# Opening loads, the joint between feed-forward and second attention, and the last routing rearranged in a one-core transformer kernel

## The reference, cut to what matters

```python
x = L0_attn_x                       # (2, 512, 512): 1024 tokens, 8 tiles of 128
x = layernorm(x + L0_attention(x))  # 32 query heads of 128, 8 key/value heads, window 128, rope
x = layernorm(x + W_down(silu(x @ W_gate.T) * (x @ W_up.T)))        # hidden width 1376
x = layernorm(x + L1_attention(x))  # 32 query heads of 16, 8 key/value heads, causal, rope
x = layernorm(x + moe(x))

def moe(x):                         # 1024 tokens, E = 8 experts, top 2, lora rank 16
    h = x @ gw1.T + gb1             # width 32
    h = relu(normalise(h) * ln_gamma + ln_beta)
    gates = h @ gw2.T + gb2         # width 8: the second gate layer
    top_v, top_i = top_k(gates, 2)
    share = softmax(top_v)
    counts = number of tokens of each expert, for each of the two choices
    w = one_hot(top_i) * share * (counts <= capacity)
    low = einsum('ni,eir->enr', x, lora_A) * w      # width 8 * 16
    return x @ weight.T + low @ lora_B / 16
```

## Time and profile before

| what | value |
|---|---|
| median of 3 runs | 1286.29 us (1282.94 to 1286.7) |
| the profiled execution's own time | 1286.41 us |
| its span | 1284.6 us |
| PE busy | 1199.4 us, 93% |
| DVE busy | 810.6 us, 63% |
| ACT busy | 749.7 us, 58% |
| POOL busy | 544.0 us, 42% |
| mean granted clock of TensorE | 0.969 |

### The profile page before, as it was taken

One profiled execution on the slowest core, in us unless ns is written; L12 is line 12 of the kernel. 1 busy time (PEld: TensorE's weight loads), 2 busy tenths in 40 slices (PEclk: granted clock), 3 DMA queues, 4 the chain that ended last, 5 costly groups with the idle time before them and its releaser, 6 DMA issues. The chain is left out here.

```text
span 1284.6 us, 21017 instructions
## 1 busy us (share of the span) xinstructions
PE 1199.4 (93%) x6674; PEld 1036.9 (81%) x6674; DVE 810.6 (63%) x2534; ACT 749.7 (58%) x1739; POOL 544.0 (42%) x503
## 2 busy tenths in 40 slices
PE   6799999999999999999996999999597999999994
PEld 4688888888888888888875788878486999999883
DVE  7657776677766677666775322211655888888657
ACT  6456765566655666566653444400217999999423
POOL 4544453445543544435423233300334666676300
PEclk9899999999999999999999899999797999999997
DMA  4311110111100111011001122100201223210001
GB/s 156 105 34 41 34 34 27 35 34 34 37 24 27 42 30 46 25 26 42 2 1 33 33 73 73 57 1 1 76 22 51 49 47 105 53 39 20 1 1 66
DMA packets 30927, 52.43 MB, mean 41 GB/s; under 512 B 5728, under 2 KB 6624, under 8 KB 30816
## 3 DMA queue, kind: packets, MB, share of 16 engines
q1 hardware_dynamic: 30240, 50.02, 13.4%
q10 hardware_dynamic: 576, 1.05, 0.2%
HBM read 39.51 MB, written 2.10 MB: 32 GB/s over the span
## 5 line engine op out<-in xcount | busy, mean ns | idle before, releaser
L407 POOL TENSOR_TENSOR turned<-turned,sin 128x512 f32<-128x512 f32 x73 | 94.5, 1294 | 316.2 <-ACT turned L285 316.2
L301 ACT ACTIVATE probs<-probs,neg_max 128x256 f32<-128x256 f32 (+1 forms) x256 | 119.8, 473 | 15.8 <-DVE neg_max L493 15.8
L1335 ACT ACTIVATE a_probs<-a_probs,a_neg_max 128x512 f32<-128x512 f32 (+3 forms) x256 | 123.5, 573 | 0.0
L1536 DVE CUSTOM_DVE_ANT_0 a_probs<-bank,a_mask 128x512 f32<-128x512 f32 (+3 forms) x256 | 109.7, 484 | 1.4 <-PE bank L1737 1.1
L93 PE MATMUL bank<-wo_hi,oT_hi 128*128 128x512 f32 x256 | 101.0, 395 | 4.4 <-DVE oT_lo L555 4.4
L626 PE MATMUL bank<-xT_hi,wq_hi 128*128 128x512 f32 x256 | 102.0, 398 | 2.1 <-DVE first_by_cos L466 2.1
L410 POOL TENSOR_TENSOR turned<-turned,by_cos 128x512 f32<-128x512 f32 x73 | 100.8, 1381 | 5.7
L626 PE MATMUL bank<-xT_lo,wq_hi 128*128 128x512 f32 x256 | 100.8, 394 | 0.0
L626 PE MATMUL bank<-xT_hi,wq_lo 128*128 128x512 f32 x256 | 100.5, 393 | 0.0
L93 PE MATMUL bank<-wo_hi,oT_lo 128*128 128x512 f32 x256 | 100.4, 392 | 0.0
L93 PE MATMUL bank<-wo_lo,oT_hi 128*128 128x512 f32 x256 | 100.4, 392 | 0.0
(11 more groups left out here) (252 smaller groups left out, 3618.5 us busy)
## 6 DMA issues: line engine op xcount, KB each, us to landing
staged<-weights SPq DMA_DIRECT2D x76, 256.0 KB, 2.8
f_staged<-weights_f SPq DMA_DIRECT2D x33, 256.0 KB, 2.7
a_q_stack<-a_qT_hi SPq DMA_DIRECT2D x64, 64.0 KB, 2.0
rows<-x_rows SPq DMA_DIRECT2D x1, 2048.0 KB, 9.4
a_k_stack<-a_kT_hi SPq DMA_DIRECT2D x64, 32.0 KB, 2.0
a_q_stack<-a_qT_lo SPq DMA_DIRECT2D x32, 64.0 KB, 2.0
out<-rows SPq DMA_DIRECT2D x8, 256.0 KB, 2.0
rows<-x_T ACTq DMA_DIRECT2D x4, 256.0 KB, 5.3
```

The lines of the kernel that those rows point to most:

```text
L301: act.activation(probs[:, s % 2, h, 0:width], probs[:, s % 2, h, 0:width], ACT.Exp, bias=neg_max[:, s % 2, h:h + 1], scale=SCALE0, accum_o ...
L407: pool.tensor_tensor(at, at, sin[:, :], ALU.mult).then_inc(sin_done, 1)
L1335: act.activation(row_probs(s, qt), row_probs(s, qt), ACT.Exp, bias=neg_max[:, h, qt:qt + 1], scale=-1.0).then_inc(exp_done, 1)
L1536: dve.tensor_tensor_reduce(row_probs(s, qt), ps_s[bank][:, at:at + seen], mask[:, SEQ - seen:SEQ], -SCALE1, HIGHEST, ALU.add, ALU.min, neg ...
```

## The change

1. Opening: blocks 7 to 10 get a buffer of their own, `first_out`, which lies over the part of `wo_hi` that is filled later; SP issues their loads behind block 6 without a wait, ahead of the wait for `xT_lo_done` and of the load of `rows`. ACT waits for `rope_lo` 7 instead of 8. DVE runs `rope_low(0, 7)` and `low_values(0, 3)` ahead of `normalise(0, 1)`.
2. Joint: a new class `Ahead` places the tensors that both blocks share. In the down phase SP loads the query/key/value weights, tables and mask over the dead gate and up inputs, ACT and POOL split them, and the norm of tiles 0 to 6 runs tile by tile, one behind the matmuls; PE transposes tiles 0 to 5 between down tiles, into the space of the hidden tiles already used. The add and norm of tile 7, and the transposes of 6 and 7, are in `attention1`, whose list on PE now starts with the projection of tile 0.
3. Routing: bias, statistics, scaling run per tile (`gate_rows`, `gate_root`, `gate_scale`), the relu'd h is transposed for four tiles at a time, and the second gate layer is one PE matmul per half against a 128x32 block matrix. Top 2 and counts are per half (`choose`). `main(1)` moves behind the count matmuls, and `low` is scaled in halves. `small` is loaded with `main`.

```diff
-FIRST_PIECES = 7
+FIRST_PIECES, FIRST_OUT = 7, 7
...
+            if m >= FIRST_OUT:
+                return first_out[:, m - FIRST_OUT, :]
...
             def first_load(m):
-                if m >= FIRST_IN_PROBS + 2:
+                if FIRST_IN_PROBS + 2 <= m < FIRST_OUT:
                     sp.wait_ge(weight_lo_done, m - 1)
-                arrived = first_in[m] if m < FIRST_IN_PROBS else weight_in[m % 2]
+                arrived = first_in[m] if m < FIRST_IN_PROBS else weight_in[m % 2] if m < FIRST_OUT else out_in
...
-            first_load(6)
-            first_load(7)
+            for m in range(6, HEAD_START):
+                first_load(m)
             sp.wait_ge(xT_lo_done, 2 * KC)
             sp.dma_start(rows[:, :, :], x_rows.rearrange("(t p) d -> p t d", p=P)).then_inc(rows_in, 16)
-            for m in range(8, HEAD_START):
-                first_load(m)
...
-            act.wait_ge(rope_lo, 8)
+            act.wait_ge(rope_lo, FIRST_PIECES)
...
-            normalise(0, 1)
             rope_low(0, 7, True)
             low_values(0, 3)
+            normalise(0, 1)
...
+class Ahead:
+        self.at, self.weights_at, self.banks = at, weights_at, banks
+        self.xT = put("xT", [P, KC, 2, TOK], at, F32R)
+        self.xT_hi, self.xT_lo = self.xT[:, :, 0, :], self.xT[:, :, 1, :]
...
+    def add_row(self, dve, rows, norm, tile):
+        dve.wait_ge(self.y_ready, tile + 1)
+        dve.tensor_tensor(rows[:, tile, :], self.banks[tile % 2][:, :], rows[:, tile, :], ALU.add).then_inc(self.y_added, 1)
+        dve.wait_ge(self.y_added, tile + 1)
+        norm.take(dve, tile)
+        norm.moments(dve, tile)
...
+            sp.wait_ge(up_ready, 2 * F_TILES)
+            for k in range(KC):
+                sp.dma_start(ahead.raw[:, k, :], w_qkv[k]).then_inc(ahead.weight_in[k], 16)
+            sp.dma_start(ahead.cos[:, :, :], cos_in).then_inc(ahead.constants_in, 16)
+            sp.dma_start(ahead.sin[:, :, :], sin_in).then_inc(ahead.constants_in, 16)
+            sp.dma_start(ahead.mask[:, :], mask_in).then_inc(ahead.constants_in, 16)
...
+            for k in range(KC):
+                act.wait_ge(ahead.weight_in[k], 16)
+                act.activation(ahead.w_hi[:, k, :], ahead.raw[:, k, :], ACT.Copy).then_inc(ahead.w_hi_done, 1)
+            for tile in range(TILES - 1):
+                if tile >= 1:
+                    next_norm.high(act, tile - 1)
+                next_norm.root(act, tile)
...
+            for k in range(KC):
+                pool.wait_ge(ahead.w_hi_done, k + 1)
+                pool.tensor_tensor(ahead.w_lo[:, k, :], ahead.raw[:, k, :], ahead.w_hi[:, k, :].bitcast(F32),
+                                   ALU.subtract).then_inc(ahead.w_lo_done, 1)
...
-            for tile in range(TILES):
-                dve.wait_ge(y_ready, tile + 1)
-                dve.tensor_tensor(rows[:, tile, :], ps_y[tile % 2][:, :], rows[:, tile, :],
-                                  ALU.add).then_inc(y_added, 1)
-                dve.wait_ge(y_added, tile + 1)
-                next_norm.take(dve, tile)
+            for tile in range(TILES - 1):
+                ahead.add_row(dve, rows, next_norm, tile)
+                if tile >= 1:
+                    next_norm.split_low(dve, tile - 1)
+                next_norm.scale(dve, tile)
...
+                if 1 <= tile < TILES - 1:
+                    next_norm.turn(pe, tile - 1)
...
+        norm = t["norms"][1]
-        ps_q, ps_kv, ps_part = psum[0:2], psum[2:4], psum[6:8]
+        ps_q, ps_kv, ps_part = psum[2:4], psum[6:8], psum[4:6]
...
+        ps_hT = [psum[1][:, 0:P], psum[6][:, 0:P]]
+        ps_gates = [psum[1][:, P:P + 4 * EXPERTS], psum[6][:, P:P + 4 * EXPERTS]]
+        ps_count = psum[6][:, 2 * P:2 * P + 2 * EXPERTS]
...
-            norm.on_scalar(act, transposed=False)
-            high_weight(0)
-            for tile in range(TILES):
-                if tile < KC - 1:
-                    high_weight(tile + 1)
-                act.wait_ge(norm.turned, tile + 1)
-                act.activation(xT_hi[:, :, tile * P:(tile + 1) * P], norm.bank(tile), ACT.Copy).then_inc(norm.hi_done, 1)
-
+            norm.root(act, TILES - 1)
...
+                if tile < 2:
+                    norm.high(act, TILES - 2 + tile)
...
+            def gate_root(tile):
+                act.wait_ge(var_ready, tile + 1)
+                act.activation(dev[:, tile:tile + 1], h_moments[:, tile, 1:2], ACT.Sqrt,
+                               bias=norm.eps[:, 0:1]).then_inc(dev_done, 1)
+
+            def turned_gates(part):
+
+                act.wait_ge(gate_steps, 2 * part + 1)
+                act.activation(hT[:, part, :], ps_hT[part], ACT.Relu).then_inc(hT_done, 1)
...
+                if tile >= 3:
+                    gate_root(tile - 3)
...
+            turned_gates(0)
+            gate_root(TILES - 3)
             norm2.high(act, TILES - 1)
             low_rows(TILES - 2)
+            gate_root(TILES - 2)
             low_rows(TILES - 1)
-            act.wait_ge(var_ready, 1)
-            act.activation(dev[:, :], var[:, :], ACT.Sqrt, bias=norm.eps[:, 0:1],
-                           scale=1.0 / GATE_H).then_inc(dev_done, 1)
-            act.wait_ge(gap_ready, 1)
-            act.activation(share[:, 1, :], gap[:, :], ACT.Exp).then_inc(share_done, 1)
+            gate_root(TILES - 1)
+            turned_gates(1)
+            act.wait_ge(choice_done, 3)
+            act.activation(share[:, 1, :], gap[:, :], ACT.Exp).then_inc(dev_done, 1)
...
-            weights(range(KC))
...
-            norm.on_vector(dve)
+            ahead.add_row(dve, rows, norm, TILES - 1)
+            norm.scale(dve, TILES - 1)
...
+                if tile < 2:
+                    norm.split_low(dve, TILES - 2 + tile)
...
+            def gate_rows(tile):
+                dve.wait_ge(side_ready, tile + 1)
+                dve.tensor_tensor(h[:, tile, :], ps_side[tile % 2][:, 0:GATE_H], names["gb1"], ALU.add).then_inc(h_copied, 1)
+                dve.wait_ge(h_copied, tile + 1)
+                step(dve.bn_stats(h_stats[:, tile, :], h[:, tile, :]))
+                dve.bn_aggr(h_moments[:, tile, :], h_stats[:, tile, :]).then_inc(var_ready, 1)
+
+            def gate_scale(tile):
+                dve.wait_ge(dev_done, tile + 1)
+                step(dve.reciprocal(dev[:, tile:tile + 1], dev[:, tile:tile + 1]))
+                step(dve.tensor_scalar(h[:, tile, :], h[:, tile, :], h_moments[:, tile, 0:1], dev[:, tile:tile + 1],
+                                       ALU.subtract, ALU.mult))
+                step(dve.tensor_tensor(h[:, tile, :], h[:, tile, :], names["gamma"], ALU.mult))
+                dve.tensor_tensor(h[:, tile, :], h[:, tile, :], names["beta"], ALU.add).then_inc(h_done, 1)
+
+            def choose(part):
+
+                tiles = range(4 * part, 4 * part + 4)
+                some = slice(4 * part, 4 * part + 4)
+                dve.wait_ge(gate_steps, 2 * part + 2)
+                step(dve.tensor_tensor(gates[:, some, :], ps_gates[part].rearrange("p (t e) -> p t e", e=EXPERTS),
+                                       each_of(names["gb2"], 4, EXPERTS), ALU.add))
+                for tile in tiles:
+                    found = dve.max(top[:, tile, :], gates[:, tile, :])
+                step(found)
+                for tile in tiles:
+                    found = dve.max_index(top_index[:, tile, :], top[:, tile, :], gates[:, tile, :])
+                step(found)
+                step(dve.tensor_copy(top_at[:, some, :], top_index[:, some, :]))
+                dve.tensor_tensor(gap[:, some], top[:, some, 1], top[:, some, 0], ALU.subtract).then_inc(choice_done, 1)
+                for n in range(2):
+                    found = dve.tensor_tensor(chosen[:, n, some, :], each_column(top_at[:, some, n], EXPERTS, 4),
+                                              each_of(names["index"], 4, EXPERTS), ALU.is_equal)
+                step(found)
+                dve.tensor_reduce(count[:, part, :, :].rearrange("p n e -> p (n e)"),
+                                  chosen[:, :, some, :].rearrange("p n t e -> p n e t"), mybir.AxisListType.X,
+                                  ALU.add).then_inc(choice_done, 1)
...
+            dve.wait_ge(main_in, 48)
+                if tile >= 3:
+                    gate_scale(tile - 3)
             norm2.split_low(dve, TILES - 2)
             gate_rows(TILES - 3)
+            choose(0)
+            gate_scale(TILES - 3)
             norm2.split_low(dve, TILES - 1)
             gate_rows(TILES - 2)
+            gate_scale(TILES - 2)
             gate_rows(TILES - 1)
...
+            gate_scale(TILES - 1)
+            choose(1)
...
+            for part in range(2):
+                some = slice(4 * part, 4 * part + 4)
+                by_expert = low[:, some, :].rearrange("p t (e r) -> p (t e) r", r=RANK)
+                dve.tensor_tensor(by_expert, by_expert,
```

(71 more changed lines are left out.)

189 lines of the change are left out of this document (77 added, 112 removed).

## The result

The changed kernel takes 1256.12 us (median of 4 runs, 1254.46 to 1256.77) against 1285.32 us for the kernel before on the same chip (4 runs, 1282.94 to 1286.7): ratio 0.9774, 95% interval 0.9758 to 0.9791. The forecast was 1257, the range 1251 to 1265. The profiled span fell by 30.5 us, 1284.6 to 1254.1; the forecast sum was 30.0.

What follows compares the result with a forecast made beforehand. PE was taken as the bound wherever it is fed, so its starved places were summed: 2.7 + 19.3 + 8.0 = 30.0 us off 1286.4 gives 1256.4, said as 1257; range 1251 to 1265.

Steps and rivals of the forecast that it cites:

- Opening: At PE's wait for the first `pT_lo`: PE goes on at 58.4 instead of 61.07 us, saving 2.7 us.
- Joint: Down phase into second attention's projections: tile 7 rotated at 939.5 instead of 958.79 us, saving 19.3 us.
- the 837 forecast: Down phase: sign that the load of `weights_qkv` is issued near 837 us.
- The clock's share: Down phase into projections: some 5 of the 19.3 us saved are the half clock.
- Closing: Routing before the last stage: first last add at 1258.1 instead of 1266.14 us, saving 8.0 us.
- the third end (C): Last routing: relu brings table loads of 1.28 us, saving only 4.2; as rival 2.6 us on PE, 1259, chance 0.08.
- D: Second attention's block starts slowly: 2.48 us on issue and 3.8 lost to half clock; 1262, chance 0.12.
- E: Down phase into projections: tile 7's norm, held by POOL, keeps `v_done` late; some 10 us saved there, 1266, chance 0.04.
- F: The 64 attention slots in new places get longer, making the kernel slower: 1288 at 0.5 us each; chance 0.03.
- B: The opening's half clock disappears too: 1253.5 us, chance 0.11.
- There are three: Whole kernel: PE starves in three places: first `pT_lo`, behind the down phase, before the last stage.
- four stretches of half clock: Whole kernel: PE's clock is at 0.50 in four longer stretches, each behind an idle time of PE.

Runs made afterwards that it cites:

- e4: Changed kernel with one added wait: POOL's four opening subtractions start only after DVE's normalise of slot 1; ratio 0.9741 to the kernel before.
- e1: Kernel before with the opening's part of the change alone; ratio 0.9971 to the kernel before.
- e3: Kernel before with the joint's part alone (norm tile by tile and projection weights in the down phase); ratio 0.9858 to the kernel before.
- e2: Kernel before with the last routing's part alone (gate layer on PE, tiles and halves); ratio 0.9940 to the kernel before.
- e10: Kernel before with only DVE's new opening order and ACT's wait for seven low halves, blocks loaded as before; single time 1289.72 us.
- e8: Changed kernel with the norm's roots, scaling, transposes and halves back in the second attention's block, weights still loaded ahead; ratio 0.9867 to the kernel before.

## Why the prediction held, step by step

- **Opening, 2.7 forecast.** PE's wait fell by 2.6 us to 5.6 (5.5 forecast), for the reason given: ACT free at 54.0 (53.9), DVE's scalings 4.65 us (4.3) held by POOL. e4 shows the hold. Too small was the whole: tile 7 of e1 is 3.95 us earlier, as a half-clock stretch at 655 to 662 went, and that in the opening shrank from 10.3 to 6.8 us. I had left the clock as it was.
- **Joint, 19.3 forecast.** e3 shows 18.7 and tile 7 came at 936.35 (936.8 with the opening). The six sets of transposes lie between down tiles, the block switch costs 0.47 (0.5). The 0.6 us that are missing are the transposes: from the first to the last down matmul it is 62.56 us (835.68 to 898.24) instead of 59.70 (839.52 to 899.22), so the six sets cost 2.9 us and not 2.2. `weights_qkv` are issued at 833.31; the 837 forecast had nothing taken off for the opening, by which the down phase begins 3.8 us earlier. No wait over 0.5 us is left there and the clock is full in the window of 896.6 to 940. The clock's share was right too: over windows of 3.4 us, busy time of PE times the missing share of the clock is 5.5 us from 900 to 935 in the kernel before, nothing now.
- **Closing, 8.0 forecast.** 8.03, in e2 as in the whole. That it fits to 0.03 us is luck in part: errors of the terms cancel. The terms: the main behind `side(5)` starts 5.86 us behind `main(0)` where it was 4.61, so 1.25 late (1.4); gate 1 adds 0.88 between `main(4)` and `main(5)` (1.0), of which 0.37 are a wait, `choose(1)` takes 2.2 (2.3), the counts don't wait and take 0.37 (0.7), the weights and the scaling lie under `main(1)`, the low transposes start at once. Behind them 1.07 us of wait for `f_low_T_lo` are left: from the first low transpose to the first add it is 3.07 us (2.6). So the three terms ahead came out 0.6 shorter and the tail 0.5 longer. The relu brought no table load, so the third end (C) fell.
- **Rivals.** D fell: the switch took 0.47 and the clock stayed. E fell: no wait for `v_done` in tiles 1 to 3. F fell: from tile 7 to `main(0)`, all 64 slots and the output projection, it is 271.79 before, 271.85 after, 271.41 in e3. B, that the opening's half clock vanishes, holds in neither kernel; 3.4 us of it are left even in e4 (0.53 from 56.8 to 60.2).
- **The places.** "There are three" was wrong, and so were four stretches of half clock. From 698 to 706 us the kernel before has a fourth wait, 8.2 us for `rows` (the norm ahead of the feed-forward), as long as the longest of the three, and behind it PE at half clock, from 703.8 to 717.4 us in windows of 3.4 us. The change leaves both as they are (8.3 us, and the clock at 0.50 from 700.4 to 714.0), so the forecast lost nothing by it; a reader who looks for the next step does.
- **The sum** was 30.0 against 30.5 by the spans and 29.2 by the medians. The opening brought 1.3 more than its term and the joint 0.6 less.

What is open: why the same instructions meet a half-clock stretch in one profile and not in another (e2 against the kernel before at 931; e10 had one at 230 us as well, e4 and e8 one at 22 to 27). No run here separates that. The wait of 2.9 us for the first exponentials, which holds an ACT table load of 1.28 us, was not tried. Nor was the largest place left, the 8.3 us and the half clock at the start of the feed-forward: they look like what the joint had before this change, a norm of all tiles ahead of the first product, but no run shows that the same cure works there.

## What to carry to other kernels

Sum a change like this from marks (the start of one instruction behind each part), not from busy shares: each part then has its own number, and here the joint and the closing part alone kept theirs (18.7 and 8.03 us), while the opening brought more. Where two chains meet at a joint, what moving both brings can't be read off one: at the first product the two halves brought nothing and 4.5 us alone and 9.4 together. List all waits by length before naming the places: one of 8.3 us was passed over here. And look at what stands ahead of a late instruction on its own engine before making anything faster: two moved lines (POOL's work behind DVE's, the relu ahead of a copy) were worth 4 us.

## What the runs showed of the hardware

- DVE's scaling of 128x256 in SBUF, 0.35 us by itself, takes 1.16 us beside POOL's subtractions and 0.41 with them put off (1.62 for four).
- A relu between roots and copies on ACT took 0.27 us and no table load; the load came with the exponential, 1.28 us.
- The granted clock differs between profiles of the same instructions (e2 and the kernel before, alike up to there): 0.51 and 1.00 in the same 3.4 us, with 11 and 25 matmuls done. One such stretch moves a single profile by 1.7 us.
- An ACT copy of 0.57 us, added to slots in which PE is busy 197.7 of 200 us and ACT 187.9, cost 0.45 us of the span.
